# How far the matmuls trail the dequantized weight groups in a transformer layer: lag of 5 groups or of 3

## The reference

```python
def _dequant(q, s):                       # s has one row per 128 rows of q
    scale_full = jnp.repeat(s, q.shape[0] // s.shape[0], axis=0)
    return (q.astype(s.dtype) - 8.0) * scale_full
Wg, Wu, Wd = _dequant(gate_q, gate_s), _dequant(up_q, up_s), _dequant(down_q, down_s)
g = jnp.einsum('bsh,hi->bsi', x, Wg)      # x: [1, 8192, 4096], Wg and Wu: [4096, 11008]
u = jnp.einsum('bsh,hi->bsi', x, Wu)
y = jnp.einsum('bsi,ih->bsh', jax.nn.silu(g) * u, Wd)   # Wd: [11008, 4096]
```

## Time and profile before

| | |
|---|---|
| median of 2 runs | 7767.77 us (7760.41 to 7775.14) |
| the profiled execution | 7767.42 us |
| span of its slowest core, core 0 | 7765.9 us (the other cores 7741.6 to 7760.9 us) |
| mean granted TensorE clock, core 0 | 0.864 |
| TensorE busy with matmuls | 6065.0 us, 78% |
| VectorE busy | 3339.8 us, 43% |
| ScalarE busy | 1086.3 us, 14% |
| HBM traffic | 1367 MB, 176 GB/s over the span |

### The profile page before, as it was taken

The page is one execution under the profiler, slowest core; times in us unless marked ns, Lnnn a source line. Parts: engine busy times, 40 slices in busy tenths (PEclk is TensorE's granted clock), DMA queues, the critical chain, the costliest instruction groups (busy, mean ns, idle before and its releaser), DMA issues.

```text
span 7765.9 us, 106026 instructions; the slowest of 8 cores (7741.6 to 7765.9 us)
## 1 busy us (share of the span) xinstructions
PE 6065.0 (78%) x31087; PEld 2685.1 (35%) x31087; DVE 3339.8 (43%) x5936; ACT 1086.3 (14%) x1887; POOL 0.2 (0%) x4
## 2 busy tenths in 40 slices
PE   3666666666788648888888888886888888888888
PEld 2333333333344323333333333332333333333333
DVE  3111212121111245555555555554555555555555
ACT  5233333334222110000000000001000000000000
POOL 0000000000000000000000000000000000000000
PEclk6777777777899769999999999997999999999999
DMA  4110110110323557777777688885777777778887
GB/s 166 55 43 34 44 44 33 44 44 11 109 98 109 178 191 232 231 238 225 229 236 230 219 253 257 257 257 187 226 230 225 234 225 233 226 218 253 255 255 245
DMA packets 631945, 1374.36 MB, mean 177 GB/s; under 512 B 39408, under 2 KB 56304, under 8 KB 610032
## 3 DMA queue, kind: packets, MB, share of 16 engines
q1 hardware_dynamic: 621040, 1334.03, 55.1%
q10 hardware_dynamic: 10368, 33.56, 1.1%
HBM read 1333.87 MB, written 33.55 MB: 176 GB/s over the span
## 4 chain that ended last, share of the span: by engine, by line
PE 53%; DVE 4%; DMA 3%; issue 3%; ACT 1%; DVEq 0%; SPq 0%; ACTq 0%
PE ps_a L1110 33%; PE ps_a L1292 15%; PE ps_x L1057 3%; DVE deq L1082 2%; PE ps_x L1245 2%; DMA out<-outp 1%; DVE hbuf L1152 1%; DMA r2c<-r 1%; DMA ring<-dq 1%; DVE sts L165 1%; ACT xlt L200 0%; DVE deq L1269 0%; DMA ssl<-dsr 0%; DVE ssb L1193 0%; PE ps_o L1057 0%
## 5 line engine op out<-in xcount | busy, mean ns | idle before, releaser
L1110 PE MATMUL ps_a<-xl,deq 128*128 128x512 bf16 x11008 | 2625.5, 395 | 0.1
L1110 PEld LDWEIGHTS ps_a<-xl,deq 128*128 128x128 bf16 x11008 | 1060.9, 101 | 1403.3 <-issue 323.3
L1082 DVE SCALAR_TENSOR_TENSOR deq<-ring,ps_x 128x512 bf16<-128x512 int32 (+1 forms) x1408 | 888.1, 672 | 1180.0 <-PE ps_o L1057 1176.9
L1292 PE MATMUL ps_a<-deq,hbuf 128*128 128x512 bf16 x5504 | 1276.9, 386 | 0.0
L1082 DVE SCALAR_TENSOR_TENSOR deq<-ring,ps_o 128x512 bf16<-128x512 int32 (+1 forms) x1408 | 883.6, 670 | 1.1 <-DMA ring<-uq 0.9
L1292 PEld LDWEIGHTS ps_a<-deq,hbuf 128*128 128x128 bf16 x5504 | 518.2, 99 | 670.8 <-issue 116.0
L1269 DVE SCALAR_TENSOR_TENSOR deq<-ring,ps_x 128x512 bf16<-128x512 int32 x704 | 452.5, 684 | 508.1 <-PE ps_o L1245 483.9
L1057 PE MATMUL ps_x<-ssb,t_e 32*128 32x512 bf16 (+1 forms) x1408 | 293.1, 410 | 416.7 <-DVE deq L1082 262.2
L627 PE MATMUL ps_o<-vaug,sgm 128*128 128x129 bf16 x2048 | 245.7, 284 | 400.4 <-ACT sgm L606 400.4
L793 PE MATMUL ps_a<-attf,wot 128*128 128x512 bf16 x2048 | 496.4, 408 | 43.3 <-ACT wot L230 43.3
L1133 ACT ACTIVATE silu<-ps_a 128x512 bf16<-128x512 f32 x172 | 89.0, 604 | 3054.1 <-PE ps_a L1110 2980.5
(11 more groups left out here) (84 smaller groups left out, 2793.9 us busy)
## 6 DMA issues: line engine op xcount, KB each, us to landing
ring<-dq SPq DMA_DIRECT2D x688, 512.0 KB
ring<-gq SPq DMA_DIRECT2D x672, 512.0 KB
ring<-uq SPq DMA_DIRECT2D x672, 512.0 KB
wqr<-wq SPq DMA_DIRECT2D x64, 1024.0 KB
wor<-wo SPq DMA_DIRECT2D x64, 1024.0 KB
xch<-xs SPq DMA_DIRECT2D x12, 2048.0 KB
xrb<-xs SPq DMA_DIRECT2D x8, 2048.0 KB
r<-r2s ACTq DMA_DIRECT2D x8, 2048.0 KB, 20.3
```

The lines of the kernel that those rows point to most:

```text
L1082: v.scalar_tensor_tensor(deq[:, dslot, 0:REG], ring[:, 2 * slot + (g % 2), 0:REG], -8.0, bcbank(bk, REG), op0=ALU.add, op1=ALU.mult).then_ ...
L1110: ins = t.matmul(ps_a[icl][:, :], deq[:, dslot, 128 * icl:128 * (icl + 1)], xl2[:, 512 * g:512 * (g + 1)], start=(g == 0), stop=(g == 31))
L1292: ins = t.matmul(ps_a[tc][:, :], hbuf[:, 512 * g + 128 * tc: 512 * g + 128 * (tc + 1)], deq[:, dslot, :], start=(g == 0), stop=(g == NG - 1))
```

## The change

Both places that hold matmuls back do so for 3 groups instead of 5. Nothing else differs.

```diff
@@ gate and up, line 1120 @@
                             pend.append((n_deq, pmm))
                             n_deq += 1
-                            if len(pend) > 5:
+                            if len(pend) > 3:
                                 emit_pmm(pend.pop(0))
```

## The result

The changed kernel is faster: 0.9803 of the kernel before, with a 95% interval of 0.9755 to 0.9851. It rests on 7580.05, 7586.10 and 7646.57 us; in the last of these, four cores took 7605 to 7645 us and the other four 7563 to 7575. The profiled execution took 7580.05 us (span 7578.5, core 0) against 7767.42 before, a ratio of 0.976; the forecast was 7592. Some executions of every kernel here ran with one die or both at a lower clock; they are left out, and where little else was there, the times of single undisturbed cores are given. A second series had 7574.6 and 7579.0 us against 7765.4 and 7772.6, so 0.975 (7576.8 / 7769.0); it has no interval on record. The mean granted clock of core 0 rose from 0.864 to 0.874.

A forecast was written before the change was run, and what follows sets the result against it. The prediction took TensorE as the bound, idle at pass heads waiting for VectorE's dequantization. Terms of 159 (99 order, 60 clock), 3 and 12 gave 174 us off 7767.4, so 7593, stated as 7592; 8-in-10 range 7555 to 7645.

The forecast's parts named there:

- The middle of a pass: nothing: Between the head and end of a pass: no change, as 1.5 us of slack stay with the lag of 3.
- The head at full clock, 1.18 us per pass: Gate and up heads: group 0's matmuls fit VectorE's wait; 1.18 us less per pass, 99 us over 84 full-width passes.
- The clock, 60 us: Up heads: matmuls in the hole keep the full clock, gate passes fall as now; 60 us of the 159 gained.
- The reasoning about the tail: End of a gate or up pass: 8 matmuls gone, 1.73 us less, against 0.55 more behind the second `pbc4`.
- Half-width blocks, 3 us: The 4 half-width passes: half as many matmuls move and VectorE sets more of the pace; 3 us gained in all.
- Down passes, 12 us: The 16 down passes: four matmuls move into the hole; 12 us better, bounds 14 us worse and 25 better.
- the 1 us that was allowed: Sign in the down passes: the wait for the output write is at most 1 us longer than 6.52.
- The rule on loop structure: TensorE at pass heads: next work at once keeps the clock, a wait drops it; without it, 60 us less gain.
- Only the order: Rival, up passes: the clock falls as often as now; 115 us gained, 7652 us; chance 0.17.
- The clock never falls: Rival, gate and up passes: group 0 holds the clock in gate passes too; 76 us more gained, 7516 us; chance 0.06.
- Low clock over a longer second block: Rival, every head: low clock covers all 16 matmuls behind the second `pbc4`; slower, 7850 us; chance 0.03.
- The turned down term: Rival, down passes: output writes tied to the weight prefetch, 14 us worse instead of 12 better, 7618 us; chance 0.14.

The follow-up runs named there:

- filler run: Kernel before, lag of 5 and order kept, plus four matmuls on data already in SBUF in the hole at every pass's head, overwritten later: 7658.73 us.
- The run with the hole kept empty: Changed kernel (lag of 3), but group 0's matmuls held back until behind the second `pbc4`: 7757.98 us, against 7760.5 and 7766.96 of the kernel before.
- The filled gap with the lag of 3: Changed kernel plus 14 matmuls on old data before the first `pbc4` of each gate pass but the first of a half: 7574.18 and 7615.54 us.

## Why the prediction was right

- *The middle of a pass: nothing.* Right. The block of 3.89 us is unchanged.
- *The head at full clock, 1.18 us per pass.* Right inside a head at full clock: 3.36 and 3.89 us came out as said. Of a whole up pass only 0.98 us was seen (37.96 to 36.98). The missing 0.2 is at its end: the next gate pass now spreads its first scales at low clock, and its first dequantization waits 1.50 instead of the 1.29 us of the row at 4099.95 in the earlier trace rows. As a mean over all passes 1.18 was too high. It counts a lost wait of about 0.3 us in each of 84 passes, but the 108 waits of the earlier trace rows are 88 long and only 20 short ones, of 0.25 to 0.73 us. The gate heads are at low clock, and gain about the 0.86 us of moved work. The filler run prices the moved work at 79 us, where the prediction had 99.
- *The clock, 60 us.* The mechanism was right, and for the up passes, on which the term was built, so was the size: 57 us. In all it was 85 us, since the gate heads, which the prediction let fall as before, gave 28 more. The two errors, 20 us too much for order and 25 too little for the clock, nearly cancel: 159 us predicted, 163.6 measured, and 71.77 us per block against 71.59 and 71.75. That the sum came so close is partly luck. A sum that comes out right did not show that its parts were; the filler run did.
- *The reasoning about the tail.* "At the end of the pass 8 matmuls are gone" was put as the source of the gain. As bookkeeping it holds, but it misleads. The run with the hole kept empty has the same tail and gained nothing. Only matmul time that lies in idle time is a gain.
- *Half-width blocks, 3 us.* Nothing measurable.
- *Down passes, 12 us.* This term was mis-sized: 28 us on core 0, beyond even its bound of 25, and 20 over the eight cores. The gap between passes hardly grew (mean of 14 on core 0: 11.50 us before, 11.60 after). The waits for output writes sum to 102.7 us in 30 times after and 101.3 in 30 before, so the earlier writes kept their lead. Of the 1.22 us per pass (mean of the cores) the filler run has 0.9 without any moved work, which I take for clock. The prediction's 12 us are 0.75 per pass: it weighed the moved work against a write tied to the prefetch, and had clock only in its upper bound, with 0.7. The Trainium skill (DMA: Bandwidth & Descriptors, "Queues, rings and completion order") has each engine alternate between the queues that it has work for. In a gap after the change, the four microseconds from the issue of the write on show only q1:

```profile
q1 hardware_dynamic: 261, 0.51, 101.7%
...
q1 hardware_dynamic: 259, 0.50, 107.0%
```

  The stretches are 7374.2 to 7376.2 and to 7378.2, and the first writes were issued at 7374.4. In the next 2 us q10 has 193 packets and q1 has 148. Over the 14 gaps of core 0 that have a prefetch beside them, the first packet of q10 starts 1.7 to 4.3 us after the issue (before the change, 1.2 to 4.3); behind the last pass of a half, with no prefetch, it starts after 0.8. Whether the write's packets had reached the engines earlier and were held back there, no row shows, so these rows neither bear out the rule nor refute it. The third addition waited 6.88 us there, 0.36 more than in the earlier trace rows, within the 1 us that was allowed.
- *The rule on loop structure* (the Trainium skill, TensorE: Matmul & The Clock Gate, "Loop structure matters more than you think"). The runs agree with it, and more strongly than the sum used it: added matmuls in a hole bought 105 us. The filled gap with the lag of 3 shows its limit, as work at once in one place only moved the fall to the next hole.
- *Rivals.* "Only the order" (7652) falls with the length of the up passes. "The clock never falls" (7516) did not come, and with the lag of 3 would not have come with the gap filled either. "Low clock over a longer second block" happened in the gate passes, where 16 matmuls took 4.73 us, but at a mean cost far from its 2.8 us. The turned down term came out the other way.

## What to carry to other kernels

Of two engines in a pipeline, look for where the bounding one waits at each restart and move its own ready work into that wait; a shorter tail pays only as far as that work fits there, and the lag must still hide the other engine's step. Where heads with the same work have two lengths, the granted clock is part of the price, and one run with idle-time filler measures it apart from the reordering. Look at every hole of a restart: with one filled and the next left half empty, the low stretch only moved here.

## What was not expected of the hardware

Four added matmuls per pass, useless for the result, made the whole kernel 105 us faster at 104 places (88 gate and up passes, 16 down passes), about 1 us for each. With the gap filled and the lag of 3, the clock fell all the same, behind the next hole. So what TensorE did in the gap did not carry it past a hole that holds four matmuls, while in the same place eight real ones kept it at 27 of 42 gate heads. And the output writes in the down gaps moved nothing for up to 4.3 us while the prefetch ran, yet the waits for them are as long in sum as before.
